# Queries and the first keys copied between SBUF tiles instead of through DRAM, in a neighbourhood attention kernel

## What is computed

```
qkv = x @ qkv_w.T + qkv_b              # 3 x 12 heads x 32 channels
scores = q . k / sqrt(32)              # each position sees a 7 x 7 window
attn = softmax([window scores, 16 register scores])
out = (attn @ [v, register v]) @ out_w.T + out_b
```

## Time and profile before

| what | value |
|---|---|
| median of 3 runs | 630.76 us |
| lowest and highest | 627.12 and 630.83 us |
| the profiled execution | 627.96 us |
| its span, first to last instruction | 626.1 us |
| PE, DVE, ACT, POOL busy in the span | 564.1, 448.5, 308.2, 292.5 us |
| moved by DMA | 94.11 MB |
| granted TensorE clock, mean | 0.992 |

### The profile page before, as it was taken

One profiled execution on the slowest core, in us unless ns is written; L12 is line 12 of the kernel. 1 busy time (PEld: TensorE's weight loads), 2 busy tenths in 40 slices (PEclk: granted clock), 3 DMA queues, 4 the chain that ended last, 5 costly groups with the idle time before them and its releaser, 6 DMA issues.

```text
span 626.1 us, 22413 instructions
## 1 busy us (share of the span) xinstructions
PE 564.1 (90%) x9227; PEld 389.5 (62%) x9227; DVE 448.5 (72%) x1009; ACT 308.2 (49%) x609; POOL 292.5 (47%) x427
## 2 busy tenths in 40 slices
PE   3669789999999999899999998998989799998998
PEld 2337666686766766567766776656667456665554
DVE  6886576887887689776778887877795887763233
ACT  1763555225543488523553246542785438644321
POOL 3105765373713866339582647326675322313131
PEclk9999999999999999899999999999997999999999
DMA  9869768795369752597537964579430011211212
GB/s 306 191 145 279 213 185 247 201 283 150 80 158 232 228 127 71 122 244 225 140 91 185 279 166 134 128 216 269 132 95 26 1 37 39 78 39 38 76 45 107
DMA packets 130637, 94.11 MB, mean 150 GB/s; under 512 B 67132, under 2 KB 124392, under 8 KB 130536
## 3 DMA queue, kind: packets, MB, share of 16 engines
q1 hardware_dynamic: 121896, 77.39, 46.7%
q0 software_dynamic: 8640, 15.30, 8.0%
HBM read 56.29 MB, written 35.54 MB: 147 GB/s over the span
## 4 chain that ended last, share of the span: by engine, by line
PE 59%; DVE 18%; DMA 8%; issue 6%; ACT 5%; POOL 2%; SPq 2%; ACTq 0%; POOLq 0%; DVEq 0%
PE ps L1173 39%; PE ps L1356 7%; PE ps L1333 4%; PE ps L1307 4%; DMA QS<-MT 4%; DVE MX L677 3%; DMA WR<-in_wqkv 2%; DMA vscr<-VT 2%; DVE ON L697 1%; DVE SUMT L690 1%; DVE RINV L696 1%; DVE X L564 1%; DMA VR<-vscr 1%; SPq L263 1%; DVE KT L539 1%
## 5 line engine op out<-in xcount | busy, mean ns | idle before, releaser
L1173 PE MATMUL ps<-XH,WQ 128*128 128x384 f16 x810 | 148.5, 333 | 15.8 <-DVE XH L510 9.6
L677 DVE TENSOR_REDUCE MX<-ps 128x2 f32<-128x372 f32 x216 | 107.8, 538 | 33.4 <-PE ps L1307 31.6
L1173 PEld LDWEIGHTS ps<-XH,WQ 128*128 128x128 f16 x810 | 76.8, 99 | 70.6 <-issue 12.5
L986 ACT ACTIVATE PT<-ps 128x448 f32<-128x448 f32 (+1 forms) x162 | 79.1, 510 | 51.3 <-PE ps L1333 50.8
L441 POOL TENSOR_TENSOR KT<-QS,KT 128x384 f16<-128x384 f32 x36 | 34.4, 963 | 94.6 <-ACT KT L1086 94.6
L1307 PE MATMUL ps<-KB,QS 120*32 120x186 f16 x1728 | 63.7, 246 | 10.4 <-issue 4.2
L1333 PE MATMUL ps<-QS,KB 122*128 122x112 f16 (+1 forms) x864 | 60.9, 213 | 8.5 <-DMA QS<-MT 4.6
L1173 PE MATMUL ps<-OS,WO 128*128 128x384 f16 x324 | 61.9, 326 | 2.3 <-DVE X L553 1.4
L1173 PE MATMUL ps<-WQ,XH 128*128 128x128 f16 x972 | 61.0, 219 | 2.3 <-issue 2.1
L382 POOL DMA_DIRECT2D QS<-MT x72 | 38.3, 536 | 50.7 <-ACT MT L976 48.5
L387 POOL TENSOR_TENSOR OS<-ON,OS 128x384 f16<-128x384 f32 x36 | 33.0, 917 | 58.6 <-ACT OS L992 58.5
(11 more groups left out here) (167 smaller groups left out, 974.8 us busy)
## 6 DMA issues: line engine op xcount, KB each, us to landing
KB<-kscr SPq DMA_DIRECT2D x108, 192.0 KB, 4.6
kscr<-KT SPq DMA_DIRECT2D x72, 192.0 KB, 2.8
VR<-vscr SPq DMA_DIRECT2D x216, 56.0 KB
QS<-qscr SPq DMA_DIRECT2D x108, 96.0 KB, 5.3
X<-in_x SPq DMA_DIRECT2D x12, 576.0 KB, 6.5
out<-X SPq DMA_DIRECT2D x11, 576.0 KB, 3.3
qscr<-QT POOLq DMA_DIRECT2D x18, 192.0 KB, 4.1
qscr<-PT POOLq DMA_DIRECT2D x18, 192.0 KB, 4.9
```

The source lines that it names most:

```text
L677: V.tensor_reduce(out=MX[:, s % 2, t, 2 * pair:2 * pair + 2], in_=ps[:, S_BANK(s, i), 0:2 * RUN].rearrange("p (h n) -> p h n", h=2), op=AL ...
L986: A(PTS[n % 4][:, 0:w], ps[:, ST_BANK(n), 0:w], ACT.Exp, scale=SCORE).then_inc(s_["exd"], 1)
L1173: last = mm(bank, lhsT(a, k), rhs(b, k), start=(k == 0 and n == 0), stop=(finish and k == steps - 1 and n == 2))
```

## The change

Three things change together. The rows of the query and key weights and their biases are put in another order on the host, so that a group's partition number is 4 x channel + head, not 32 x head + channel. Then partitions `4d` to `4d + 3` of a tile are, read in order, exactly what one partition `d` of `QS` or `KB` holds for its four heads, and one DMA can copy SBUF to SBUF. The queries of all tiles and the keys of tiles 0 and 1 (`DIRECT = 2`) are copied so, the keys strip by strip. The keys of tiles 2 to 5 still go through `kscr`, but POOL writes them now and not SP. The key slots rotate by two a group, so that tiles 0 and 1 of the next group land in the slots of tiles 2 and 3 of this one.

```
-def slot(s):
-    return s % 4
+def slot(gi, s):
+    return (2 * gi + s) % 4
+DIRECT = 2
...
             def keys_out(gi, a):                                   # SP
                 sp.wait_ge(s_["k_lo"], 6 * gi + a + 1)
                 sp.wait_ge(s_["krg"], 3 * gi + 3)
-                for part in range(2):
-                    sp.dma_start(kscr[part, :, :, a, :], KT[:, a % 3, part, :, :]).then_inc(kw_out[a % 3], 16)
+                if gi and a == 0:
+                    sp.wait_ge(s_["st_mm"], 36 * gi - 12)
+                for s in range(DIRECT):
+                    for j, part in enumerate((0, 1, 0)):
+                        sp.dma_start(KB[DH * j:DH * (j + 1), :, slot(gi, s), LEAD + CHUNK * a:LEAD + CHUNK * (a + 1)],
+                                     KT[:, a % 3, part, s, :]).then_inc(kw_out[a % 3], 16)
...
             def queries_in(gi, s):
-                sp.wait_ge(q_out[s], 16 * (gi + 1))
+                sp.wait_ge(s_["q_lo"], 6 * gi + s + 1)
                 for j, part in enumerate((0, 0, 1)):
                     sp.dma_start(QS[DH * j:DH * (j + 1), :, s * SN:(s + 1) * SN],
-                                 qscr[part].rearrange("(h d) n -> d h n", d=DH)[:, :, s * SN:(s + 1) * SN]).then_inc(qs_in[s], 16)
+                                 QTS[s % 5][:, part, :]).then_inc(qs_in[s], 16)
...
                 if 36 * gi > 0:
                     sp.wait_ge(s_["st_mm"], 36 * gi)
-                for s in range(4):
-                    keys_in(gi, s)
+                for s in range(TILES):
                     queries_in(gi, s)
-                for s in (4, 5):
-                    queries_in(gi, s)
+                    if gi and s in (1, 3):
+                        if s == 1:
+                            for i in range(3):
+                                sp.wait_ge(ks_out[i], 64 * gi + 64)
+                        keys_in(gi, 2 + s // 2)
+                if gi == 0:
+                    for i in range(3):
+                        sp.wait_ge(ks_out[i], 64)
+                    for s in (2, 3):
+                        keys_in(gi, s)
...
-            def queries_out(gi, s):
-                pool.wait_ge(s_["q_lo"], 6 * gi + s + 1)
-                pool.dma_start(qscr.rearrange("a p n -> p a n")[:, :, s * SN:(s + 1) * SN], QTS[s % 5]).then_inc(q_out[s], 16)
+            def keys_out(gi, a):                                   # POOL
+                pool.wait_ge(s_["k_lo"], 6 * gi + a + 1)
+                pool.wait_ge(s_["krg"], 3 * gi + 3)
+                for part in range(2):
+                    pool.dma_start(kscr[part, :, DIRECT:TILES, a, :], KT[:, a % 3, part, DIRECT:TILES, :]).then_inc(ks_out[a % 3], 16)
...
             for gi in range(STAGES):
-                for s in range(TILES):
-                    queries_out(gi, s)
+                for a in range(min(early_keys(gi), STRIPS - 1), STRIPS):
+                    keys_out(gi, a)
...
                         if a == 3 and s == 3 and gi < STAGES - 1:
                             register_keys(gi + 1)
+                        if gi < STAGES - 1 and (s, a) in ((4, 4), (5, 0), (5, 1), (5, 3), (5, 5)):
+                            keys_out(gi + 1, ((4, 4), (5, 0), (5, 1), (5, 3), (5, 5)).index((s, a)))
                         if a == 5 and s:
                             low_output(gi, s - 1)
...
-                if 64 * gi + 32 * (a // 3) > 0:
-                    dve.wait_ge(kw_out[a % 3], 64 * gi + 32 * (a // 3))
+                if 2 * gi + a // 3 > 0:
+                    dve.wait_ge(kw_out[a % 3], 192 * gi + 96 * (a // 3))
+                    dve.wait_ge(ks_out[a % 3], 64 * gi + 32 * (a // 3))
...
             def scores(gi, s, i):
                 if i == 0:
-                    pe.wait_ge(kb_in[slot(s)], kb_count(gi, s))
+                    if s < DIRECT:
+                        for b in range(3):
+                            pe.wait_ge(kw_out[b], 192 * (gi + 1))
+                    else:
+                        pe.wait_ge(kb_in[slot(gi, s)], kb_count(gi, s))
```

More of the change, by code:

```diff
@@ L137, in build @@
         CS = [q16[:, N:N + TOK * 96].rearrange("p (t n) -> p t n", t=TOK), ptf[:, 0:TOK * 96].rearrange("p (t n) -> p t n", t=TOK)]
-        qscr = nc.dram_tensor("qscr", [2, P, N], F16, kind="Internal").ap()
         kscr = nc.dram_tensor("kscr", [2, P, TILES, STRIPS, CHUNK], F16, kind="Internal").ap()
@@ L182, in build @@
         v_out = [sem(f"v_out{i}") for i in range(TILES)]
-        q_out = [sem(f"q_out{i}") for i in range(TILES)]
         vr_in = [[sem(f"vr_in{i}{j}") for j in (0, 1)] for i in (0, 1)]
         kw_out = [sem(f"kw_out{i}") for i in range(3)]
+        ks_out = [sem(f"ks_out{i}") for i in range(3)]
         kb_in = [sem(f"kb_in{i}") for i in range(4)]
@@ L189, in kb_count @@
         def kb_count(gi, s):
-            if s in (2, 3):
-                return 48 * (gi + 1)
-            return 96 * gi + (48 if s < 2 else 96)
+            return 48 * sum(slot(g, t) == slot(gi, s) for g in range(gi + 1) for t in range(DIRECT, TILES) if g < gi or t <= s)
         K_BANK = lambda gi, a: a % 2 if gi else (4, 6, 2, 3, 5, 7)[a]
@@ L240, in keys_out @@
                 sp.wait_ge(s_["krg"], 3 * gi + 3)
-                for part in range(2):
-                    sp.dma_start(kscr[part, :, :, a, :], KT[:, a % 3, part, :, :]).then_inc(kw_out[a % 3], 16)
+                if gi and a == 0:
[4 more added lines that the diff above has]
+                                     KT[:, a % 3, part, s, :]).then_inc(kw_out[a % 3], 16)
             def keys_in(gi, s):
                 for j, part in enumerate((0, 1, 0)):
-                    sp.dma_start(KB[DH * j:DH * (j + 1), :, slot(s), LEAD:LEAD + STRIPS * CHUNK],
-                                 kscr[part, :, s, :, :].rearrange("(h d) a n -> d h (a n)", d=DH)).then_inc(kb_in[slot(s)], 16)
+                    sp.dma_start(KB[DH * j:DH * (j + 1), :, slot(gi, s), LEAD:LEAD + STRIPS * CHUNK],
+                                 kscr[part, :, s, :, :].rearrange("(d h) a n -> d h (a n)", d=DH)).then_inc(kb_in[slot(gi, s)], 16)
             def queries_in(gi, s):
-                sp.wait_ge(q_out[s], 16 * (gi + 1))
+                sp.wait_ge(s_["q_lo"], 6 * gi + s + 1)
                 for j, part in enumerate((0, 0, 1)):
                     sp.dma_start(QS[DH * j:DH * (j + 1), :, s * SN:(s + 1) * SN],
-                                 qscr[part].rearrange("(h d) n -> d h n", d=DH)[:, :, s * SN:(s + 1) * SN]).then_inc(qs_in[s], 16)
+                                 QTS[s % 5][:, part, :]).then_inc(qs_in[s], 16)
             def values_in(gi, s):
@@ L267, in _ @@
                     keys_out(gi, a)
-                for i in range(3):
-                    sp.wait_ge(kw_out[i], 64 * gi + 64)
                 if gi == 0:
@@ L272, in _ @@
                 if gi == STAGES - 1:
+                    for i in range(3):
+                        sp.wait_ge(kw_out[i], 192 * STAGES)
+                        sp.wait_ge(ks_out[i], 64 * STAGES)
                     sp.dma_start(f2raw, fc2).then_inc(s_["f_in"], 16)
@@ L349, in register_keys @@
                 for i in range(3):
-                    if 64 * gi > 0:
-                        pool.wait_ge(kw_out[i], 64 * gi)
+                    if gi:
+                        pool.wait_ge(kw_out[i], 192 * gi)
+                        pool.wait_ge(ks_out[i], 64 * gi)
                     for part in range(2):
@@ L953, in queries_high @@
                 if s == 5:
-                    act.wait_ge(q_out[0], 16 * (gi + 1))
+                    act.wait_ge(qs_in[0], 48 * (gi + 1))
                 if 36 * gi > 0:
@@ L984, in exps @@
                 for i in ((2,), (3,), (4,), (0, 1, 5))[n] if n < 4 else ():
-                    act.wait_ge(q_out[i], 16 * (gi + 1))
+                    act.wait_ge(qs_in[i], 48 * (gi + 1))
                 A(PTS[n % 4][:, 0:w], ps[:, ST_BANK(n), 0:w], ACT.Exp, scale=SCORE).then_inc(s_["exd"], 1)
@@ L1307, in scores @@
                         last = mm(ps[32 * j:32 * j + 32, S_BANK(s, i), hh * RUN:(hh + 1) * RUN], QS[0:SROWS, h, q0:q0 + 32],
-                                  KB[0:SROWS, h, slot(s), at:at + RUN], start=True, stop=True)
+                                  KB[0:SROWS, h, slot(gi, s), at:at + RUN], start=True, stop=True)
                 last.then_inc(s_["s_mm"], 1)
@@ L1332, in key_scores @@
                 for h in range(HEADS):
-                    last = mm(ps[:, ST_BANK(n), h * w:(h + 1) * w], KB[0:TROWS, h, slot(s), LEAD + CHUNK * a:LEAD + CHUNK * (a + 1)],
+                    last = mm(ps[:, ST_BANK(n), h * w:(h + 1) * w], KB[0:TROWS, h, slot(gi, s), LEAD + CHUNK * a:LEAD + CHUNK * (a + 1)],
                               QS[0:TROWS, h, s * SN + CT_ * q0:s * SN + CT_ * q1], start=True, stop=True)
@@ L1689 @@
     member = (group[:, None] == np.arange(GROUPS)[None, :]).astype(np.float32)
-    consts = [column(qkv_b[:2 * C]), column(qkv_b[2 * C:]), column(L0_conv_out_b), column(np.asarray(L1_conv_fc1_b).reshape(-1)),
```

(8 more changed lines are left out.)

## The result

| | before | changed |
|---|---|---|
| median of 4 runs each, same chip | 628.94 us | 661.7 us |
| lowest and highest | 623.47, 630.83 | 660.21, 662.29 |
| span of the profiled execution | 626.1 us | 660.4 us |
| its own time | 627.96 us | 662.29 us |

The changed kernel is slower: ratio 1.0551, 95% interval 1.0502 to 1.0600. The forecast was 633.4 us, the range ended at 641. The page of the changed kernel gives these busy times, to be held against the earlier trace rows.

A forecast was written before the change was run, and what follows sets the result against it. PE, busy 90% of the span, was taken as the bound, leaving some 62 us idle to win. Terms -1.9 + 1.0 + 3.5 = +2.6 us gave 630.6 us, 633.4 carried over to the median; range 625 to 641.

The forecast's parts named there:

- What SP gets: Step pricing SP's six direct key copies a strip at 0.44 us an issue, 2.6 us a strip.
- the term of +1.0 us: DVE's key copies late behind SP's 18th copy: 0.8 us at the end of group 0, 0.2 at group 3.
- Rival 2: SP too slow at 0.65 us an issue: 14.2 us over four group ends, 646.6 us in all; chance 0.11.
- The landing of 2.8 us: Landing time of the old key write, taken as an upper value for a direct key copy.
- the queries' detour: Query write and read through DRAM, 4.9 + 5.3 us; removal priced at zero, covered by the remaining query products.
- one such stretch: PE at 1.2 GHz for 3.7 us behind idleness at the end of group 2; expected once more, no new one.
- The end of group 2: POOL's key scratch writes delay the norm's last low part, so PE starts keys(3, 5) 3.5 us later.
- the clash that I named and gave no term: POOL's scratch writes meeting DVE's KT copies at five group ends: 0.57 us each, +2.9 us if all meet.
- The -1.9 us for faster landings: PE waits removed: 0.74 us for maxima after group 1's start, 1.11 us for values after group 3's.
- rival 3: POOL dearer: 1.07 us an issue and DVE copies doubled at every group end, +7.2 us, 638.0 us; chance 0.14.
- Rival 1: DMA relief wins: waits for maxima, values and the unexplained ones before scores vanish, -8.0 us, 622.8 us; chance 0.10.
- rival 4: POOL's delay at the end of group 2 is swallowed, the trace mislabelling that wait: -0.9 us, 629.9 us; chance 0.20.

The follow-up runs named there:

- keys_only: Changed kernel with the queries back through DRAM, new column order kept: 664.04 us, ratio 1.0594 to the kernel before.
- pool_writes_only: Kernel before, old column order, with all scratch key writes issued by POOL in the changed kernel's places: 639.74 us, ratio 1.0187.
- queries_only: Kernel before with the new column order and the queries copied directly, all keys through DRAM as before: 628.14 us, ratio 0.9989.
- one_tile_early: one_tile_direct with POOL's strip 4 writes at the end of group 2 back before low_output(4): 628.24 us, ratio 1.0006.
- one_tile_direct: Changed kernel with only key tile 0 direct, key reads reordered, and strip 4's POOL writes behind the last low part (end of group 2): 623.98 us, ratio 0.9943.
- padded_queries: Kernel before with new column order, all through DRAM, plus a fifth unused head row in the queries' DRAM tensor: 626.45 us, ratio 1.0003.
- x_loads_moved: one_tile_late with the first two loads of the second image issued one tile earlier in group 0: 625.15 us, ratio 0.9979.
- one_tile_late: one_tile_direct with POOL's writes of strips 2, 3 and 4 at the end of group 2 behind the same step's low part: 624.44 us, ratio 0.9972.

## Why the prediction was wrong

**The step that failed** is "What SP gets", its sentence "I take 0.44". The row that I called nearest had the right number of rows and the wrong form; the measured price is 0.60 us, and 0.71 with gaps and long issues. With 0.71 in the prediction's own sum the 18th copy lands 17 x 0.71 + 2.8 = 14.9 us after SP's start, 4.6 us later than at 0.44, and everything else turns around: SP no longer follows the strips, and the term of +1.0 us becomes 5.4 + 4.8 + 4.0 + 4.0 = 18.2. Rival 2 was therefore what happened, with 0.11 of my chances and stated price 14.2 us. The landing of 2.8 us was called an upper value and was none: of the three copies that DVE waited for at the end of group 0 two took 4.06 and 3.82 us, the third 2.18.

**Rival 2's price held for the waits it named and was too small for the whole.** At the four group ends PE's QT waits are 16.9 us; the two such waits shown before were 0.82 and 0.83 us, so about 15.3 were added, against 14.2. That the two are so near is in part luck, since the same sum at the measured 0.71 us gives 18.2. Three things were missing from it:

- Group 0. I costed the queries' detour at nothing, cover the query products. But SP is in order: its 36 copies of group 0 run from 26.99 to 51.60 us, and the copy of query tile 0, on which the sixth query tile's buffer waits, stands behind them. ACT waits 6.0 us for it, PE 2.80 us for the queries, and 4.39 us for the keys of tile 2, read last of all. That is 7.2 us. The wait of ACT, `q_out` exchanged for `qs_in`, was an added wait that I did not price; but `keys_only`, without it, loses as much at the keys of tile 2, so it is rather that SP ends the key copies late, at 51.6 us, where in the kernel before its last key write ended at 44.1.
- The clock. The stops' stretches at the lower level, by the estimate above some 9.1 us of busy time. I had counted one such stretch for the end of group 2 and none for rival 2.
- A second stop at the end of group 0, 1.35 us for `keys_low`, because DVE is late there for `KU` too.

**The end of group 2** went the right way. Forecast +3.5 us (2.1 to 5.2), measured 6.39 - 1.90 = +4.5; POOL's issue is 0.75 us, not 0.9 (512 rows cost hardly more than 256), but POOL waited for DVE, which ended strip 4's copy at 283.03 us, 1.6 us later, counted from PE's products, than in the kernel before. DVE's copy of strip 3 had waited for SP's 6th copy of this group end, which landed at 277.60 us, and strip 4's then took 1.85 us beside an issue and a subtraction of POOL, where it took 1.32 beside subtractions. Meeting POOL's issues is the clash that I named and gave no term; `pool_writes_only` shows it. That the term came within 1 us is therefore in part luck.

**The -1.9 us for faster landings** came and was lost again. Both waits that it names are gone, 0.74 us for the maxima and 1.11 us for the values. But the waits for the maxima rose in all from 4.6 to 8.7 us; 3.5 of them are one wait in group 0 beside the loads of the second image. Query copies land in 2.8 to 3.4 us where write and read took 10.2, and that bought nothing, as said: `queries_only` equals the kernel before.

**POOL's queue**, rival 3, was no rival but a part: some 4 us by the medians of `one_tile_early` and `one_tile_direct`. Why `pool_writes_only` loses 13 us and `one_tile_early`, where POOL writes five tiles of six, loses nothing, stays open. Rival 1 and rival 4 are refuted for this kernel by its time. But rival 1's relief is there: the 4.2 us labelled issue before the scores and the 1.3 us for the values are missing from the lists of the changed kernel and of `one_tile_direct`, which has only 1.0 us for key reads in their place.

The Trainium skill, page DMA: Bandwidth & Descriptors, section Issuing engines are not separate DMA queues, says that issuing from several engines saves only the sequencer's time for it, "usually small relative to the DMA itself". One copy bears that out, 0.60 us of issue against 2.0 us to landing. Thirty-six in a row do not: at the end of group 0 they took 25.66 us to issue and the last landed 2.0 us after its issue, so landings overlapped and the issues set the pace.

## What to carry to other kernels

Count the issues of the busiest DMA queue per step of the pipeline and hold their sum against the step: here 3 x 0.71 = 2.1 us fits in 2.7 and costs nothing against DRAM scratch (0.9943 to 1.0006 in four kernels), 4 x 0.71 = 2.8 nearly does (1.0103, with six still in group 0), 6 x 0.71 = 4.3 loses 5%. Look for a row with the same form on both sides of the copy before pricing an issue; the same number of rows was not enough. And ask for every stop of PE that a change may bring what the clock adds to it.

## What the runs showed of the hardware

- An SP issue of 128 rows took 0.44 us (median) where both sides have the same three dimensions and 0.60 where one side has 128 even rows and the other 32 x 4, from DRAM and from SBUF alike. `padded_queries` has both prices in one kernel.
- POOL's issue for rows of 256 bytes: 0.75 us for 512 rows, 0.88 for 640 and for 768, no straight line through 0.53 (128) and 0.72 to 0.74 (256), which are for rows of 512 and 768 bytes.
- A pair of DVE copies of 672 float16 columns took 0.58 us alone and 2.48 beside two DMA issues and one subtraction of POOL. Beside issues alone a single copy took between 0.32 us, as without them, and 1.04.
- Beside loads of 576 KB in group 0 two copies of 3 KB landed in 4.2 and 6.9 us, 16 us ahead of the loads in 2.2 and 3.0 (`padded_queries`); the three key reads of a tile landed in 5.6 to 6.9 us behind such loads (`x_loads_moved`), in 3.6 to 4.5 us without them (`one_tile_late`).
